# Sums of exponentials in a context attention: three of four pairs of key tiles are added on GpSimd before their product with ones

## The reference, cut to what matters

```python
q = jnp.einsum('bsc,hcd->bhsd', xn, wq)
k = jnp.einsum('btc,hcd->bhtd', yn, wk)
v = jnp.einsum('btc,hcd->bhtd', yn, wv)
a = jax.nn.softmax(jnp.einsum('bhsd,bhtd->bhst', q, k) * D ** (-0.5), axis=-1)
...
o = jnp.einsum('bhst,bhtd->bhsd', a, v)
```

## Time and profile before

| | us |
|---|---|
| three runs | 4323.85, 4335.82, 4353.62 |
| median | 4335.82 |
| the profiled execution's own time | 4334.44 |
| its span | 4332.6 |
| mean granted clock of TensorE | 0.896 of 2.4 GHz |

### The profile page before, as it was taken

The page is one execution under the profiler, slowest core; times in us unless marked ns, Lnnn a source line. Parts: engine busy times, 40 slices in busy tenths (PEclk is TensorE's granted clock), DMA queues, the critical chain, the costliest instruction groups (busy, mean ns, idle before and its releaser), DMA issues. The chain is left out here.

```text
span 4332.6 us, 56718 instructions
## 1 busy us (share of the span) xinstructions
PE 3450.6 (80%) x21582; PEld 1893.0 (44%) x21582; DVE 2230.4 (51%) x4281; ACT 1642.5 (38%) x2455; POOL 905.5 (21%) x989
## 2 busy tenths in 40 slices
PE   3887678898887588898887788988875788946995
PEld 2423453426324345245334535264244543435884
DVE  3465766553464855734557764634648656430002
ACT  1343653342343733333345642423437433401221
POOL 0110542101201722011104512012006320120002
PEclk9889789999899799999898798999998899958997
DMA  4111102201202011111102012011120011034553
GB/s 80 37 55 59 16 7 74 62 19 36 67 12 73 1 42 61 41 35 42 55 20 54 1 42 83 19 40 42 50 73 1 30 66 48 30 115 155 173 175 119
DMA packets 244259, 239.67 MB, mean 55 GB/s; under 512 B 111902, under 2 KB 209420, under 8 KB 241548
## 3 DMA queue, kind: packets, MB, share of 16 engines
q1 hardware_dynamic: 234224, 217.91, 16.7%
q10 hardware_dynamic: 6684, 9.63, 0.7%
q0 software_dynamic: 3072, 8.39, 0.6%
HBM read 167.20 MB, written 68.68 MB: 54 GB/s over the span
## 5 line engine op out<-in xcount | busy, mean ns | idle before, releaser
L857 ACT ACTIVATE prob<-psum 128x1024 f32<-128x1024 f32 x384 | 372.2, 1021 | 559.1 <-PE psum L777 559.1
L1184 ACT ACTIVATE prob<-psum 128x1024 f32<-128x1024 f32 (+3 forms) x384 | 331.6, 914 | 443.7 <-PE psum L1104 443.7
L898 DVE TENSOR_REDUCE scr<-psum 128x1 f32<-128x512 f32 x576 | 371.4, 685 | 216.7 <-PE psum L764 212.9
L1222 DVE TENSOR_REDUCE stats<-psum 128x1 f32<-128x512 f32 (+3 forms) x576 | 334.3, 620 | 165.7 <-PE psum L1092 161.0
L1104 PE MATMUL psum<-stack 32*128 32x512 f32 (+3 forms) x1536 | 213.3, 626 | 63.2 <-ACT prob L1184 33.1
L774 PE MATMUL psum<-stack 32*128 32x512 f32 x1536 | 228.6, 665 | 33.2 <-DVE xo L888 24.7
L395 PE MATMUL psum<-ident 128*128 128x128 f32 x1736 | 220.2, 287 | 14.6 <-PEq L1809 9.6
L395 PEld LDWEIGHTS psum<-ident 128*128 128x128 f32 x1736 | 214.3, 203 | 24.7 <-issue 23.9
L805 PE MATMUL psum<-prob,ones_f 128*32 128x512 f32 x1536 | 206.8, 606 | 0.0
L1119 PE MATMUL psum<-prob,vbig 128*32 128x512 f32 (+3 forms) x1536 | 194.4, 580 | 4.3 <-ACT prob L1184 4.3
L2676 PE MATMUL psum<-xgT,ew 128*128 128x256 f32 x736 | 167.0, 386 | 18.0 <-DVE xgT L2722 18.0
(11 more groups left out here) (444 smaller groups left out, 6690.6 us busy)
## 6 DMA issues: line engine op xcount, KB each, us to landing
ew<-in_L_ffn_W SPq DMA_DIRECT2D x46, 1024.0 KB, 7.5
stack<-q_terms SPq DMA_DIRECT2D x144, 128.0 KB, 2.4
w_mlp<-in_L_xattn_a_li_w SPq DMA_DIRECT2D x16, 1024.0 KB, 7.3
q_terms<-parts SPq DMA_DIRECT2D x96, 128.0 KB, 2.1
stack<-k_terms SPq DMA_DIRECT2D x72, 128.0 KB, 2.7
w_mlp<-k_terms SPq DMA_DIRECT2D x36, 256.0 KB, 4.4
w_mlp<-a_terms SPq DMA_DIRECT2D x36, 256.0 KB, 4.9
a_keys<-stack SPq DMA_DIRECT2D x4, 2048.0 KB, 6.3
```

The lines of the kernel that those rows point to most:

```text
L857: act.activation(prob[:, i % 4, :, :], psum[:, 2 * p:2 * p + 2, :], ACT.Exp, scale=scale).then_inc(exped, 1)
L898: dve.tensor_reduce(found[:, c:c + 1], ring(i), AX.X, ALU.max).then_inc(freed, 1)
L1184: act.activation(prob[:, i % 4, :, q0:T], psum[:, 2 * p:2 * p + 2, q0:T], ACT.Exp, scale=scale).then_inc(exped, 1)
L1222: dve.tensor_reduce(found[:, c:c + 1], ring(i)[:, 0:keys_of(t)], AX.X, ALU.max).then_inc(freed, 1)
```

## The change

In e2 (and only there: `paired` is 0 in e1) key tiles 0 to 5 of each group are taken in three pairs. GpSimd adds the exponentials of the two tiles of a pair, in two instructions of 128x1024, into `pairs`, a single buffer of 4 heads that lies in `parts2`. TensorE multiplies the ones by that sum instead of by each tile: the sum of tiles 0 and 1 in step 3, of 2 and 3 in step 5, of 4 and 5 in step 7. Tiles 6 and 7 keep their own products with ones. `added_two` tells TensorE and ScalarE that a half of a pair is added, `pair_read` tells GpSimd that the buffer may be written again. `weighed` now comes from the value product in steps 0 to 5. The exponentials have eight slots, four steps deep: `prob` and two more steps in memory of `cT`, `cnT`, `xh` and `xT`, which become parts of `c_pair` and `x_pair`.

```diff
-    x, xh, xa, xo = (sb(n, [P, QT, C]) for n in ("x", "xh", "xa", "xo"))
-    xT = sb("xT", [P, KT, T])
-    cT, cnT = sb("cT", [P, 1, TC]), sb("cnT", [P, 1, TC])
+    x, xa, xo = (sb(n, [P, QT, C]) for n in ("x", "xa", "xo"))
+    x_pair, c_pair = sb("x_pair", [P, 4, T]), sb("c_pair", [P, 2, TC])
+    xh = x_pair[:, 0:2, :].rearrange("p a (b n) -> p (a b) n", n=C)
+    xT = x_pair[:, 2:4, :]
+    cT, cnT = c_pair[:, 0:1, :], c_pair[:, 1:2, :]
...
+    four_steps = [prob[:, 2 * i:2 * i + 2, :, :].rearrange("p a b n -> p (a b) n") for i in range(2)]
+    four_steps += [c_pair[:, :, :].rearrange("p a (b n) -> p (a b) n", n=T), x_pair[:, :, :]]
+    pairs = parts2[:, 0:8 * T].bitcast(F32).rearrange("p (j n) -> p j n", n=T)
...
+        paired = 0 if terms is None else n_keys // P // 2 - 1
...
+                        elif paired:
+                            last = pe.matmul(o, lhsT, four_steps[n % 4][:, j, :], start=first_, stop=final, skip_group_check=True)
                         else:
                             pe.matmul(o, lhsT, prob[:, slot, j % 2, :], start=first_, stop=final, skip_group_check=True)
+                    if kt < 2 * paired:
+                        last.then_inc(weighed, 1)
 
                 def add_up(n):
                     g, kt = steps[n]
+                    if paired and kt >= 3 and kt % 2:
+                        m = paired * g + (kt - 3) // 2
+                        pe.wait_ge(added_two, 2 * m + 2)
+                        for j in range(J):
+                            last = pe.matmul(psum[W * j:W * j + W, 7, :], ones_f[:, :], pairs[:, j, :],
+                                             start=(kt == 3), stop=False, skip_group_check=True)
+                        last.then_inc(pair_read, 1)
+                    if kt < 2 * paired:
+                        return
                     for j in range(J):
-                        last = pe.matmul(psum[W * j:W * j + W, 7, :], ones_f[:, :], prob[:, (2 * n + j // 2) % 4, j % 2, :],
-                                         start=(kt == order[0]), stop=(kt == order[-1]), skip_group_check=True)
+                        weights = four_steps[n % 4][:, j, :] if paired else prob[:, (2 * n + j // 2) % 4, j % 2, :]
+                        last = pe.matmul(psum[W * j:W * j + W, 7, :], ones_f[:, :], weights,
+                                         start=(not paired and kt == order[0]), stop=(kt == order[-1]), skip_group_check=True)
                     last.then_inc(weighed, 1)
...
+                        if paired:
+                            if n >= 4:
+                                act.wait_ge(weighed, n - 3)
+                                g4, kt4 = steps[n - 4]
+                                if kt4 < 2 * paired:
+                                    act.wait_ge(added_two, 2 * (paired * g4 + kt4 // 2) + p + 1)
+                            act.activation(four_steps[n % 4][:, 2 * p:2 * p + 2, :], psum[:, 2 * p:2 * p + 2, :], ACT.Exp,
+                                           scale=scale).then_inc(exped, 1)
+                            continue
...
+                if paired:
+                    pool.wait_ge(stored, stored_of_group * (HG - 1))
+                for g in range(HG if paired else 0):
+                    for m in range(paired):
+                        n = kts * g + 2 * m + 1
+                        if paired * g + m:
+                            pool.wait_ge(pair_read, paired * g + m)
+                        for p in range(2):
+                            pool.wait_ge(exped, 2 * n + p + 1)
+                            heads = slice(2 * p, 2 * p + 2)
+                            pool.tensor_tensor(pairs[:, heads, :], four_steps[(n - 1) % 4][:, heads, :],
+                                               four_steps[n % 4][:, heads, :], ALU.add).then_inc(added_two, 1)
```

More of the change, by code:

```diff
@@ L683, in whole_heads @@
         with stage(nc, tag, "projected", "taken", "split_by_pool", "stored", "placed_a", "placed_b", "measured", "freed",
-                   "dc", "pads_zero", "split", "scored", "exped", "masked", "weighed", "lifted", "divided") as (
+                   "dc", "pads_zero", "split", "scored", "exped", "masked", "weighed", "lifted", "divided", "added_two", "pair_read") as (
                 block, projected, taken, split_by_pool, stored, placed_a, placed_b, measured, freed,
-                dc, pads_zero, split, scored, exped, masked, weighed, lifted, divided):
+                dc, pads_zero, split, scored, exped, masked, weighed, lifted, divided, added_two, pair_read):
             placed = (placed_a, placed_b)
```

## The result

The change made the kernel slower: 4399.25 us, median of 4 (4372.5 to 4429.7), against 4338.8; the recorded ratio, which is not the quotient of the two medians, is 1.0157, 95% interval 1.0122 to 1.0191. A second measurement of the same kernel beside 23 runs of before gave 4411.97 against 4328.6, 1.0189 (1.0165 to 1.0214). I had forecast 4321. The profiled execution took 4414.98 us with a span of 4413.0, 80 us more than before.

A forecast was written before the change was run, and what follows sets the result against it. TensorE bounds steps with maxima, ScalarE's chain the last group. Per batch element -3.4 - 4.0 + 3.6 + 0.6 = -3.2 us, four times -12.8, plus -1.4 for half-clock starts: -14.2, giving 4321 us (64%), range 4303 to 4341.

The forecast's parts named there:

- the two engines' shared interface: GpSimd contends with VectorE instructions having two SBUF inputs; little such work in e2, so additions nearer 2.13, gain 2.4 us larger.
- the signs that I had named: Prediction wrong if TensorE waits for sums inside the loop, maxima exceed 686 ns, or ScalarE starts over 1.40 us after score.
- rival 4: Less busy TensorE in the last head group drops to granted clock 0.5: +37 us, 4372; 3%.
- Rival 3: GpSimd sets the step through the single sums buffer, from 3.3 us an addition; at 4.3, 4381 us; 4%.
- The additions' price: Each GpSimd addition of 128x1024 in e2 takes 2.48 us, with ends 2.13 and 2.97.
- pairs fit: Two additions, 4.96 us, fit the loop's 6.6 us with maxima or 5.7 in group 3, except once at the end.
- forecast 0.6: TensorE's wait for the sums of tiles 4 and 5 in the last group: 0.6 us a batch element.
- the chain of 3.39: ScalarE's score-to-exponentials chain, 3.39 us a step, limits group 0's steps 1, 2 and 4 and all of group 3.
- the 3.55 of VectorE: VectorE's maxima and reciprocal limit steps 0 to 2 of groups 1 and 2 to 3.55 us, from 4.21.
- the second ones product: Extra product in step 7: 0.97 us in groups 0, 1 and 3, 0.72 in group 2, together +3.6.
- the ring: Eight exponential slots instead of four cost and give nothing by themselves; they make room for GpSimd's reading.
- a tail of 2.4: TensorE's wait for the last sums at the stage's end, 0.6 us in each of four batch elements.

The follow-up runs named there:

- the run with zeros: The change plus bfloat16 products of a zero tile on TensorE where it starves, at group switches and after step 4's value product in groups 1 and 2: 4386.68 us, 1.0130.
- short additions: The change with each GpSimd addition cut from 512 columns a head to 4, leaving the sums incomplete: 4310.64 us against 4331.26, 0.9954.
- the version with the multiplication later: The change with GpSimd waiting for the small operations before adding tiles 4 and 5, and VectorE's multiplication moved from step 3 to 4: 4313.59 us, 0.9968.
- the probe: The kernel before plus a separate stage timing ten kinds of VectorE instruction on 128x128, alone and beside GpSimd additions of 128x1024; no kernel time given.

## Why the prediction was wrong

- **The step that failed** is the one on the two engines' shared interface, under GpSimd. I weighed the rule only for what VectorE does to the additions, found one multiplication in the earlier trace rows worth naming, and concluded that the gain might be larger. The other direction, what an addition of 2.35 us does to VectorE's instructions, I priced at nothing and did not name. The small operations that prepare the maxima, 0.17 us each, the prediction does not mention. They lasted 1.40 and 2.27 us at the switches, and the multiplication of 0.69 us 2.36 to 2.78. This term is missing from the sum: at most 14.5 us a loop by the run with zeros. The rule as I told it speaks of two SBUF inputs only; the instruction held longest at the switch is a copy to bfloat16, with one. None of the signs that I had named could show it: the maxima still take 686 ns, ScalarE still starts 1.40 us after a score product (861.73 to 863.13), and TensorE waits for no sum before the stage's end.
- **What it set off** I had as rival 4, with 3% and the wrong cause. Lower activity in the last group did nothing to the clock (1.00 from 958.3 us to the end of the loop). The starving in the first three groups did: at least 12.1 us a loop. Rival 3 (GpSimd sets the step) had the right engine and the wrong mechanism: its cycle was not the limit, 2.35 us an addition against the 3.3 from which it decides.
- **What stood.** The additions' price (2.35 us, where I took 2.48) and that pairs fit; TensorE waits 0.21 us for GpSimd at the end of the first loop, forecast 0.6; the chain of 3.39, the 3.55 of VectorE (3.45 to 3.74), the second ones product (5.18 to 6.03 in the step behind the switch, 0.85 where I had 0.97), nothing from the ring. With short additions all of it can be read: 4331.26 - 20.6 us, where I had forecast -14.2 with a tail of 2.4 that is absent there. The forecast was near for a kernel without the hold, and the version with the multiplication later, 0.9968, is 14 us faster than before (15.0 by the medians).

## What to carry to other kernels

Before giving GpSimd a long elementwise instruction, list VectorE's instructions that would fall beside it, the shortest ones too: here those with two SBUF inputs, and SBUF to SBUF copies and tensor_scalars, did not end before the GpSimd addition that was already under way, from 128x16 to 128x512 elements. Put such additions behind the group of small operations by a semaphore, which the runs here bear out; feeding the small ones from PSUM is what the probe suggests, and no run tried it in the kernel. And when TensorE starves behind such a wait, count the half clock that comes with it: here it was at least 12.1 of 26.6 us a loop.

## What the runs showed of the hardware that I had not expected

- A VectorE instruction of 128x16 elements (0.17 us) lasted up to 2.27 us beside a GpSimd addition of 128x1024. The reciprocal, also from SBUF to SBUF, kept its 0.94 to 0.95 us.
- The hold works both ways: beside a multiplication of VectorE an addition of 128x512 that had started 0.02 us later took 1.79 us instead of 1.27 (up to 1.80 over the run).
- Halving the additions left a chain of small held instructions as slow (switch 11.75 against 11.83 us) and let the single long one through in two groups of three.
- One wait of TensorE, of 4.36 us (851.6 to 855.9), came with 6.8 us at a granted clock of 0.50 (853.5 to 860.3); with products of zeros in its place, there was no such stretch.
